# Four shared expert groups moved into the last steps of a decoder kernel, with a new order of all queues

## The reference

```python
x = x + attn(layernorm(x))           # softmax(att * tril(k=-1)): masked scores count as 0, not as -inf
x = x + xattn(layernorm(x), ctx)     # q = x @ W.T + b; softmax(q @ ctx.T) @ ctx
n = layernorm(x)
scores = softmax(n @ gate_w.T)       # 8 experts; top 2 of scores + gate_bias
y = sum(mlp(n, w1[e], w2[e], w3[e]) * combine[:, e]) + mlp(n, sw1, sw2, sw3)
x = x + y                            # mlp: (silu(n @ w1.T) * (n @ w3.T)) @ w2.T, inner size 256
```

## Time and profile before

| | us |
|---|---|
| median of three runs | 857.41 (856.18 to 861.7) |
| the profiled execution, time | 864.15 |
| the same, span from first to last instruction | 862.4 |

### The profile page before, as it was taken

One profiled execution on the slowest core, in us unless ns is written; L12 is line 12 of the kernel. 1 busy time (PEld: TensorE's weight loads), 2 busy tenths in 40 slices (PEclk: granted clock), 3 DMA queues, 4 the chain that ended last, 5 costly groups with the idle time before them and its releaser, 6 DMA issues.

```text
span 862.4 us, 16767 instructions
## 1 busy us (share of the span) xinstructions
PE 713.2 (83%) x5504; PEld 527.8 (61%) x5504; DVE 512.3 (59%) x1292; ACT 431.6 (50%) x958; POOL 445.9 (52%) x684
## 2 busy tenths in 40 slices
PE   1468989999899898998989999889881889889963
PEld 0233556767667676676666767666771778778753
DVE  0243565787876877768787787786765332222216
ACT  2123446656566475655756557556551245455530
POOL 4023445466656665566665666546544225555540
PEclk9956689999999999999999999999996899999987
DMA  9743554636637356373663735502210212222164
GB/s 253 134 97 65 122 143 95 160 85 141 162 76 172 87 139 166 72 173 88 136 163 76 172 97 129 149 1 91 90 52 19 53 44 75 75 72 69 38 175 124
DMA packets 121411, 93.36 MB, mean 108 GB/s; under 512 B 9682, under 2 KB 112999, under 8 KB 121200
## 3 DMA queue, kind: packets, MB, share of 16 engines
q1 hardware_dynamic: 116976, 83.83, 41.2%
q0 software_dynamic: 4352, 8.47, 2.9%
HBM read 54.30 MB, written 38.08 MB: 107 GB/s over the span
## 4 chain that ended last, share of the span: by engine, by line
PE 40%; DVE 23%; DMA 14%; SPq 8%; issue 6%; POOL 4%; ACT 3%; another core or an unknown queue 2%; DVEq 0%; POOLq 0%; ACTq 0%
DMA qst<-q_parts 7%; DMA k_stack<-parts 6%; PE banks L288 6%; DVE mx L1282 5%; PE banks L957 4%; PE banks L310 3%; DVE xn L1252 3%; PE banks L239 3%; PE banks L686 3%; PE banks L723 2%; DVE mq L1297 2%; PE banks L688 2%; SPq L585 2%; PE banks L299 2%; DVE xmax L1311 2%
## 5 line engine op out<-in xcount | busy, mean ns | idle before, releaser
L1162 ACT ACTIVATE prob<-banks 128x512 f32<-128x512 f32 x192 | 115.1, 600 | 107.8 <-PE banks L723 54.8
L1589 POOL TENSOR_SCALAR_AFFINE_SELECT prob<-prob 128x256 f32<-128x256 f32 (+1 forms) x192 | 91.2, 485 | 84.7 <-ACT prob L1162 84.5
L1282 DVE TENSOR_REDUCE mx<-banks 128x2 f32<-128x512 f32 x128 | 87.3, 682 | 53.9 <-PE banks L688 44.4
L957 PE MATMUL banks<-info,xprobT 128*128 128x128 f32 (+1 forms) x832 | 103.8, 275 | 0.1
L957 PEld LDWEIGHTS banks<-info,xprobT 128*128 128x128 f32 (+1 forms) x832 | 99.3, 192 | 1.0 <-issue 0.5
L1278 DVE TENSOR_REDUCE mx<-banks 128x4 f32<-128x512 f32 x64 | 44.3, 692 | 82.8 <-PE banks L681 79.9
L1613 POOL DMA_INDIRECT sorted_rows<-row,place x64 | 65.2, 1018 | 47.0 <-DVE place L1434 32.2
L483 DVE TENSOR_TENSOR xprobT<-banks,xprob 128x512 f32<-128x512 f32 x36 | 24.9, 692 | 87.1 <-ACT xprob L381 63.8
L1311 DVE TENSOR_REDUCE xmax<-banks 128x1 f32<-128x896 f32 x64 | 62.7, 980 | 19.0 <-PE banks L919 13.5
L1053 ACT COPY xprobT<-banks 128x512 f32<-128x512 f32 (+2 forms) x128 | 64.6, 504 | 17.8 <-PE banks L939 17.8
L939 PE MATMUL banks<-cst,xprob 128*128 128x128 f32 (+1 forms) x416 | 68.0, 277 | 1.4 <-ACT xprob L1041 1.3
(11 more groups left out here) (186 smaller groups left out, 1709.8 us busy)
## 6 DMA issues: line engine op xcount, KB each, us to landing
sorted_rows<-pad SPq DMA_DIRECT2D x33, 520.0 KB, 8.6
infoT<-in_ctxT SPq DMA_DIRECT2D x16, 800.5 KB
info<-in_ctx SPq DMA_DIRECT2D x16, 448.0 KB
kst<-k_stack SPq DMA_DIRECT2D x32, 192.0 KB
info<-in_ctx SPq DMA_DIRECT2D x16, 320.0 KB
q_parts<-parts SPq DMA_DIRECT2D x32, 96.0 KB, 2.6
k_stack<-parts SPq DMA_DIRECT2D x32, 96.0 KB, 2.6
qst<-q_parts SPq DMA_DIRECT2D x32, 96.0 KB
```

What stands on the lines that cost most here:

```text
L957: mm = pe.matmul(ps[:, V_BANK, u * P:(u + 1) * P], lhsT=xprobT[hf][0:w, m - blocks[0], :], rhs=info[0:w, m, :], start=(m == blocks[0]), st ...
L1162: act.activation(prob[n % 2][:, kind * 512:(kind + 1) * 512], ps[:, G_BANK, :], ACT.Exp, scale=SCALE).then_inc(s["p_exp"], 1)
L1282: dve.tensor_reduce(mx[:, 1, h:h + 2], bank.rearrange("p (c n) -> p c n", c=2), AX.X, ALU.max).then_inc(s["alpha_max"], 1)
L1589: pool.affine_select(out=w, in_=w, compare_op=ALU.is_gt, fill=0.0, base=0, pattern=[[0, 4 if kind == 2 else 2], [1, P]], channel_multiplie ...
```

## The change

It has five parts.

1. The first four shared groups run inside steps 17 and 18 (with their last instructions in the following step) by new calls `early_up`, `early_down`, `early_hi`, `early_lo`, `early_silu`, `early_hidden` and `early_add`, in PSUM banks 5, 6 and 7. After the sorted part only groups 4 to 7 remain; their first two casts are made before it, and VectorE puts `add_back` of groups 0 to 3 between them.
2. The rest of x, w2 and the spare rows are queued by SP in later steps, and blank rows three steps later; GpSimd's four memsets of `vaug` and `kst` move into its first working step.
3. The units of sequence 0's alpha pass alternate between two banks (5 and 6).
4. The order of all five `step` lists is new. They are also cut at another point: what stood at the head of the next step now stands at the end of this one.
5. The routed rows are laid out so that a partition's four rows of a group are neighbours in memory: 2 KB per read in place of 512 B. Token rows are numbered p * 32 + t in place of t * 128 + p.

```diff
+                for t in range(GT):
+                    for z in range(2):
+                        mm = pe.matmul(ps[:, Y_BANKS[1], t * D:(t + 1) * D], lhsT=h[g % 2][z][:, t * P:(t + 1) * P],
...
+            def early_up(g, z):
+                if g is None:
+                    return
+                pe.wait_ge(s["x3_lo_done"], g + 1)
+                if 2 * g + z:
+                    pe.wait_ge(s["h_done"], 2 * g + z)
+                else:
+                    pe.wait_ge(s["alpha_max"], 12 * B)
+                    pe.wait_ge(s["p_exp"], 12 * B)
+                    pe.wait_ge(s["w13_lo_done"], B)
+                for half_w in range(2):
+                    w = slice(half_w * INTER + z * P, half_w * INTER + (z + 1) * P)
+                    for n, (a, b) in enumerate(((w13_hi, x3_hi), (w13_lo, x3_hi), (w13_hi, x3_lo))):
+                        mm = pe.matmul(ps[:, EARLY_BANKS[half_w], :], lhsT=a[:, E, w], rhs=b[g % 2], start=(n == 0), stop=(n == 2))
+                mm.then_inc(s["up_ps"], 1)
...
-                shared(0, EARLY)
                 pe.wait_ge(s["slots_done"], 1)
...
-                act.activation(sil[z], ps[:, 2 * z, :], ACT.Silu).then_inc(s["silu_done"], 1)
+                act.activation(sil[z], ps[:, EARLY_BANKS[0] if g < EARLY else 2 * z, :], ACT.Silu).then_inc(s["silu_done"], 1)
...
-                shared(0, EARLY)
+                shared_hi(EARLY)
+                shared_hi(EARLY + 1)
                 sorted_hi(0)
...
-                shared(EARLY, NGR)
-                for g in range(NGR):
+                for g in range(EARLY, NGR):
+                    for z in range(2):
+                        hidden(g, z)
+                    if g > EARLY:
+                        add_shared(g - 1)
+                    if g >= EARLY + 2:
+                        add_back(2 * (g - EARLY - 2))
+                        add_back(2 * (g - EARLY - 2) + 1)
+                add_shared(NGR - 1)
+                for g in range(2 * (NGR - EARLY - 2), NGR):
                     add_back(g)
...
-                for g in range(2, EARLY):
+                for g in range(EARLY, EARLY + 2):
                     shared_lo(g)
...
+        def early(i, n):
+            g = 2 * (i - B - 1) + n
+            return g if 0 <= g < EARLY else None
+        def bank_of(b, u):
+            return G_BANK if b == 0 and u % 2 else A_BANK
...
+            def later_inputs(i):
+                if i == 0:
+                    sp.dma_start(xall[:, 2 * T:NT, :], xt[:, 2 * T:NT, :]).then_inc(s["x_in"], 16)
+                elif i == 2:
+                    sp.dma_start(w2_sb[:], w2).then_inc(s["w2_in"], 16)
+                elif i == 3:
+                    sp.wait_ge(s["pad_done"], 2)
...
-            home_tiles = dy.rearrange("(k t p) d -> p k t d", k=TOPK, p=P)
+            home_tiles = dy.rearrange("(k p t) d -> p k t d", k=TOPK, p=P)
...
-                after(pe, "alpha_max", 12 * b + u)
-                bank = ps[:, A_BANK, :]
+                after(pe, "alpha_max", 12 * b + u - (b == 0))
+                bank = ps[:, bank_of(b, u), :]
...
+                cross_scores(j, 0)
+                values(g, 3)
+                early_down(early(i, 0))
+                cross_transposes(k, 3, 1)
+                maxima_T(i)
+                early_up(early(i, 1), 1)
+                cross_values(k, 3)
...
+                residual(j)
+                info_low(k, 1)
+                row_inputs(l - 1)
+                cross_weight(l)
+                send_rows(l - 1)
+                deviation3(l)
```

More of the change, by code:

```diff
@@ L341, in rest @@
                 shared(EARLY, NGR)
-            return rest
+            return early_up, early_down, rest
         def moe_act(act):
@@ L353, in shared_hi, with early_hi, early_silu @@
                 act.copy(x3_hi[g % 2], x3T[:, g * GN:(g + 1) * GN]).then_inc(s["x3_hi_done"], 1)
+            def early_hi(g):
+                if g is not None:
+                    shared_hi(g)
+            def early_silu(g, z):
+                if g is not None:
+                    silu(g, z)
             def silu(g, z):
@@ L517, in rest, with early_lo @@
                     sorted_home(j)
-                for g in range(EARLY, NGR):
+                for g in range(EARLY + 2, NGR):
                     shared_lo(g)
-            return shared_lo, rest
+            def early_lo(g):
+                if g is not None:
+                    shared_lo(g)
+            return early_lo, rest
         block = stack.enter_context(nc.Block())
         STEPS = range(-2, B + 5)
+        def early(i, n):
+            g = 2 * (i - B - 1) + n
+            return g if 0 <= g < EARLY else None
         KINDS = (2, 0, 1)
@@ L1018, in step @@
                 gamma(g, 11)
-                ranks(i)
+                cross_scores(j, 0)
[5 more added lines that the diff above has]
+                cross_values(k, 3)
+                out_T(g, 0)
+                alpha(f, 0)
+                early_down(early(i, 1))
+                out_T(g, 1)
+                gamma(i, 0)
+                cross_transposes(j, 0, 0)
+                cross_scores(j, 1)
+                cross_transposes(j, 0, 1)
+                cross_values(j, 0)
             for i in STEPS:
@@ L1437, in step @@
                 f, g, j, k, l = i + 1, i - 1, i - 2, i - 3, i - 4
+                early_hidden(early(g, 1), 0)
+                places(l - 1)
+                early_add(early(g, 0))
+                heads_out(j, 1)
+                cross_max(k, 0)
+                early_hidden(early(g, 1), 1)
+                head_sums(j, 0)
+                cross_add(l)
+                head_sums(j, 1)
+                cross_max(k, 1)
+                alpha_max(i, 0)
+                statistics3(l)
+                value_heads(i)
+                head_rec(j)
+                alpha_max(i, 1)
+                normalised1(f)
                 alpha_max(i, 2)
                 normalised3(l)
-                normalised1(f)
                 alpha_max(i, 3)
```

249 lines of the change are left out of this document (122 added, 127 removed).

## The result

| | before | changed |
|---|---|---|
| median | 859.56 us (856.18 to 861.77, 4 runs) | 907.8 us (896.68 to 913.92, 4 runs) |
| profiled execution, its span | 864.15, 862.4 us | 904.99, 903.3 us |
| mean granted clock | 0.939 | 0.884 |

The ratio is 1.048, with a 95% interval of 1.037 to 1.059. The forecast was 823 us (range 802 to 843), with 0.04 for slower. The ratio leaves out the two slower executions of the changed kernel (910.61 and 913.92 us), which the median of four holds.

A forecast was written before the change was run, and what follows sets the result against it. TensorE was taken to set the full step (busy 32.9 of 36.0 us). Start -7, full steps -14, early groups 0 and end -13.5 sum to -34.5 us, 4.0%, giving 823 us; range 802 to 843.

The forecast's parts named there:

- Full steps: Twelve full steps: fewer TensorE waits through new engine orders, 1.2 us each, -14 us in all.
- The stack comes about 4 us earlier: Full steps, SP: without infoT in front the stack lands sooner, saving 0.38 us per step.
- The 0.83 us per step: Full steps, TensorE: wait behind an exponential at gamma 1 nearly goes, with cross work of half 1 placed before it.
- The bound "0 and -37": Range for the full steps: from no gain to 12 x 3.1 us gained.
- Slower: Rival, chance 0.05: late second piece of info_lo stalls TensorE each full step; at 3 us late, 873 us.
- The clock: Rival, chance 0.14: the filling runs at 2.4 GHz, 19.5 us less, about 804 us.
- Start: Pipeline filling: inputs queued later and two banks for the first maxima pass, -7 us, bounds -3 and -27.
- the four memsets "at nothing": Start, GpSimd: memsets moved behind the first deviation cost nothing, up to 1.5 us if late.
- Early groups: Four shared groups moved into two thin steps: sorted part's gain offset by 11 us growth, net 0, bounds -6 and +9.
- Ten table loads: Early groups, ScalarE: ten activation table loads where there were two, one counted on the chain, 0.9 us beyond its cover.
- the drain: Skill page's 1380 ns beside each table load; by its 2.66 us, eight added switches would be 21 us of ScalarE.
- End: Last shared groups and adds: casts made before the sorted part, adds between groups, -13.5 us, bounds -9 and -16.

The follow-up runs named there:

- b_end: Kernel before with only the change's end (early casts, adds between groups, 2 KB row reads): 857.15 us against 870.98, ratio 0.987.
- a_sp_before: Changed kernel with SP's old order of transfers put back: 886.34 us against 871.87 for the kernel before, ratio 1.014.
- a_sp_lock: Changed kernel with SP's old order and GpSimd's first `info_low` moved ahead of `cross_diff`: 864.4 us against 867.95 for the kernel before, ratio 0.994.
- a_lock: Changed kernel with only GpSimd's first `info_low` moved ahead of `cross_diff`, SP's changed order kept: 895.23 us against 870.98 for the kernel before, ratio 1.027.
- a_parts_lock: Changed kernel with GpSimd's `info_low` move, and both halves of parts and stacks ahead of the maxima rows on SP: 832.34 us against 870.98, ratio 0.959.
- a_late_groups: a_parts_lock with the first four shared groups back after the steps: 830.64 us, ratio 0.956 to the kernel before.
- after: The changed kernel as first measured and profiled: median 907.8 us against 859.56 for the kernel before, ratio 1.048.
- after_again: The changed kernel run once more, unaltered, in a later comparison with the kernel before: ratio 1.048.
- repaired_again: The same kernel as a_parts_lock, run once more on one chip with the kernel before: 856.05 us, ratio 0.985.

## Why the prediction was wrong, by its own steps

- **Full steps, forecast -14 us, measured +74.7, of which profiles of one kind show 43 to 56.** This step failed. "The stack comes about 4 us earlier" was wrong: it was issued 1.9 us sooner after the maxima transposes (9.8 in place of 11.7) and landed as late as before, since the 1 MB of blank rows and the info half still stood ahead of it. The parts themselves did land in 2.3 us in place of 3.8. The 0.83 us per step that I took for the exponentials at gamma 1 bought nothing either: where they are gone under the old lists as well (b_end), TensorE comes 1.4 us sooner and the wait for the stack is 18.8 us in nine steps in place of 3.8. A wait removed ahead of a transfer is a wait for that transfer. The bound "0 and -37" had no end on the loss side, and none of my rows excluded one.
- **GpSimd beside VectorE, not priced at all.** The sum has no term for it; it measured 1.25 us of VectorE and 1.3 us of TensorE's wait in every full step, and 1.6 us of the step once it was repaired (38.0 to 36.4, a_sp_before to a_sp_lock). The rival *Slower* looked at the right engine and at `info_low`, but asked when its second piece would be ready. What counted was the first piece, and whom it ran beside. The show such an instruction of 1.28 us; that one of 2.09 us would fall on VectorE's choice was to be read from the two lists, as both it and the choice follow VectorE's minimum (`cross_min`, `cross_diff`).
- **The clock.** I priced it at the filling, on the gain side. It counted in the steps, against me: the waits of 1.8 and 2.3 us for the stack at 419.50 and 258.20 us were followed by 4 us at 0.60 and 0.50. Before, with waits of at most 1.5 us, it stood at 1.00.
- **Start, -7 us.** Wrong in time, though small in the sum. The first maxima transposes came 7.7 us earlier, but the first alpha only 1.15, because the four memsets "at nothing" cost 4.8 us through VectorE. In time the start is worth 0.5 us by the medians (the ratio's interval is -4 to +1 us): the next sequence's stack stops TensorE at 52.45 us, and the filling ran at 0.56, not above 0.61.
- **Early groups, 0 us.** Right. The sorted part did start 5.2 us after SP's first sorted load (757.37 to 762.61; forecast some 6), and the thin steps took back what that gave. Ten table loads were there, of 1.28 us each, with 0.1 us of idle time in all ahead of the four for silu; the drain did not show.
- **End, -13.5 us.** Right: -13.3 in the profile, and 11.5 us (1.3%) by b_end.

The loss is two causes that do not add: from 1.048 the late stack's repair alone leads to 1.014, the lock's alone (GpSimd's instruction no longer beside the choice) to 1.027, both to 0.959 or 0.985. In the profile of a_lock the step is as long as in the changed kernel's first (40.5 us), since its wait for the stack is 3.0 us in place of 2.1. With one of the two left, the granted clock over the steps is 0.97 (a_sp_before) or 0.90 (a_lock); with both repaired it is 1.00. How long a gap must be for that no run shows: the kernel before stands at 1.00 with waits of up to 1.5 us.

## What to carry to other kernels

Reordering one engine changes what runs beside what on all the others: before pricing a moved GpSimd instruction at nothing, list what VectorE does in the same microseconds. In an in-order pipeline the time at which a transfer is wanted moves with every wait that is removed ahead of it, so compute its landing and its new due time together. Where TensorE is over 90% busy, price a new gap above its length: 3.0 us of wait cost 5.5 us of step (a_lock), 1.3 us cost 1.6 (a_sp_before). And before a difference between two profiles is put down to the change, look at a stage that the change does not touch: here the sorted part was 17 us shorter, and the steps were to be compared with another profile.

## What the runs showed of the hardware

- Some VectorE instructions stand until the GpSimd instruction beside them ends. Two SCALAR_TENSOR_TENSOR of 128x8 took 0.37 us beside a 0.20 us instruction of GpSimd (a_sp_lock), 0.93 in the kernel before (beside `masked`) and 2.18 or 2.62 beside a 2.09 us TENSOR_TENSOR of GpSimd, the same in every full step; two TENSOR_SCALAR of 128x128 took 0.60 us alone and 5.40 beside the four memsets. Each ended within 0.2 us of GpSimd's. The Trainium skill's page "GPSIMD Engine Reference" (1. Specifications) states the cause: the SBUF interfaces are shared, with contention for VectorE instructions that have two SBUF inputs or run in a two-port mode. The traces agree, and show that it lasts until GpSimd's instruction ends. A kernel with the memsets elsewhere was not tried; by the rows it would gain up to 4.8 us at the first alpha.
- The ratios of one kernel differ by where it was timed (0.959 and 0.985 for the repaired one). In 15 of the 20 profiles ScalarE has 10 to 26 idle stretches with no releaser in the trace, 17 to 56 us in all, in the steps and in the sorted part, which then takes 124 to 130 us from its first up to its last down; in the five others (the changed kernel's first, a_lock, a_parts_lock, a_late_groups, b_end) it has none and the sorted part takes 107 to 109. Neither the kernel nor the chip decides: after and after_again are one kernel, as are a_parts_lock and repaired_again, and after_again ran on the chip of a_lock. What they are stays open.
